# Decoder layer with latent attention, WKV and experts: the hand-over to the experts in a written order, first loads on POOL's queue, four half buffers for single z

## The reference, cut to what matters

```python
x = x + attention(layernorm(x))            # 16 sequences x 128 tokens x 256, 16 heads, latent 72, causal
x = x + sigmoid(layernorm(x)) * wkv(ctx)   # two scans over time of exp(ctx), each way
x = x + experts(layernorm(x))              # 8 experts, 512 wide, two of them for each token

# attention: K = V = x @ latent_w + latent_b;  q_h = x @ Wd_w[h] + Wd_b[h]
#   z_h = softmax(mask(q_h K^T / 4)) V;  out = concat(z_h) @ out_w + out_b
# experts: scores = x @ router_w.T, best two with gates
#   out += gate_e * ((silu(x @ w_gate[e].T) * (x @ w_up[e].T)) @ w_down[e].T)
```

## Time and the profile before

| | us |
|---|---|
| median of 3 runs (lowest, highest) | 666.33 (665.54, 668.06) |
| the profiled execution, its own time | 666.71 |
| its span | 665.0 |
| TensorE busy | 558.7 (84%) |
| VectorE busy | 418.1 (63%) |
| ScalarE busy | 366.6 (55%) |
| POOL busy | 328.6 (49%) |

### The profile page before, as it was taken

One profiled execution on the slowest core, in us unless ns is written; L12 is line 12 of the kernel. 1 busy time (PEld: TensorE's weight loads), 2 busy tenths in 40 slices (PEclk: granted clock), 3 DMA queues, 4 the chain that ended last, 5 costly groups with the idle time before them and its releaser, 6 DMA issues.

```text
span 665.0 us, 11259 instructions
## 1 busy us (share of the span) xinstructions
PE 558.7 (84%) x3778; PEld 489.2 (74%) x3778; DVE 418.1 (63%) x888; ACT 366.6 (55%) x997; POOL 328.6 (49%) x300
## 2 busy tenths in 40 slices
PE   1997869998979997999689567596299999999991
PEld 0885757776758876778567446596299999999991
DVE  4468475565876739856455744778167777777760
ACT  5276545756658544645364422665167677667651
POOL 3274635625245176632533441027656777766533
PEclk9999879999999998999798888799599999999997
DMA  7234444463444322523221165547578897888710
GB/s 233 82 56 67 56 61 76 62 90 51 63 88 99 51 43 51 102 73 61 42 87 31 28 200 177 147 116 141 146 203 220 230 225 220 227 218 230 182 34 0
DMA packets 55757, 75.92 MB, mean 114 GB/s; under 512 B 11730, under 2 KB 45140, under 8 KB 55444
## 3 DMA queue, kind: packets, MB, share of 16 engines
q1 hardware_dynamic: 45098, 64.90, 39.5%
q0 software_dynamic: 9856, 10.28, 9.1%
q10 hardware_dynamic: 746, 0.02, 0.1%
HBM read 48.90 MB, written 10.40 MB: 89 GB/s over the span
## 4 chain that ended last, share of the span: by engine, by line
PE 45%; DVE 20%; issue 12%; POOL 10%; ACT 7%; DMA 4%; another core or an unknown queue 1%; SPq 0%; POOLq 0%; ACTq 0%; DVEq 0%
PE P L842 22%; PE PO L842 9%; PE PO L951 4%; DVE ZT L1391 3%; ACT EB L1143 3%; PE P L920 3%; DVE small L1380 2%; POOL EB L1712 2%; POOL xs L1748 2%; DVE arena L1413 2%; PE P L938 2%; DVE arena L1415 2%; DMA qT<-qP 1%; PE P L996 1%; DMA arena<-wd 1%
## 5 line engine op out<-in xcount | busy, mean ns | idle before, releaser
L1143 ACT ACTIVATE EB<-P,small 128x128 f32<-128x128 f32 x256 | 90.6, 366 | 120.3 <-DVE small L1380 117.7
L842 PE MATMUL P<-GT,WF 128*128 128x256 f32 x1104 | 147.8, 292 | 7.4 <-DVE GT L1290 6.0
L1712 POOL TENSOR_TENSOR EB<-EB,small 128x512 f32<-128x512 f32 x64 | 75.7, 1183 | 153.6 <-DVE small L1384 153.5
L842 PEld LDWEIGHTS P<-GT,WF 128*128 128x128 f32 x1104 | 141.3, 199 | 8.4 <-DVE GT L1290 6.6
L1772 POOL DMA_INDIRECT out<-Y,TK x46 | 74.5, 1619 | 53.5 <-ACT Y L1229 43.5
L1762 POOL DMA_INDIRECT cxa<-xd,TK x46 | 64.2, 1396 | 60.3 <-DMA TK<-xs 51.5
L938 PE MATMUL P<-PT,V 128*72 128x512 f32 x128 | 68.4, 616 | 25.7 <-DVE ZT L1391 21.2
L920 PEld LDWEIGHTS P<-KT,qT 72*128 72x128 f32 x512 | 70.6, 201 | 9.3 <-DMA qT<-qP 5.8
L920 PE MATMUL P<-KT,qT 72*128 72x128 f32 x512 | 71.3, 284 | 5.0 <-DMA qT<-qP 4.6
L951 PE MATMUL PO<-Ow,zP 128*128 128x256 f32 x288 | 74.3, 399 | 0.0
L842 PE MATMUL PO<-WF,HR 128*128 128x256 f32 x552 | 70.0, 283 | 0.0
(11 more groups left out here) (186 smaller groups left out, 942.9 us busy)
## 6 DMA issues: line engine op xcount, KB each, us to landing
arena<-wf SPq DMA_DIRECT2D x36, 512.0 KB
WR<-wf SPq DMA_DIRECT2D x33, 512.0 KB
qT<-qP SPq DMA_DIRECT2D x63, 128.0 KB
zP<-ZT SPq DMA_DIRECT2D x80, 72.0 KB
zP<-ZT SPq DMA_DIRECT2D x96, 36.0 KB
X<-x SPq DMA_DIRECT2D x4, 512.0 KB, 5.8
cxa<-ctxin SPq DMA_DIRECT2D x4, 512.0 KB, 6.1
out<-X SPq DMA_DIRECT2D x3, 512.0 KB, 3.6
```

What stands on the lines that cost most here:

```text
L842: r = e.matmul(o, lt(a), rt_(b), start=start and n == 0, stop=stop and n == 2, skip_group_check=skip)
L1143: e.activation(EB[i][:, j, :], S[:, 128 * j:128 * j + 128], ACT.Exp, bias=NM[i][:, j:j + 1], accum_out=SM[i][:, j:j + 1]).then_inc(s_exp, 1)
L1712: e.tensor_tensor(EB[i][:, :, :], EB[i][:, :, :], SM[i].unsqueeze(2).broadcast_to([128, 4, 128]), ALU.mult).then_inc(s_prob, 1)
```

## The change

- The first three weight pieces (gw) and the first three lists (gtk) are loaded from POOL's queue with semaphores of their own. `lists` waits until turn 5 x 65 and emits them together with the first three gathers (before: after plan(0) on SP, with the gathers after the last unit).
- The 24 single units use the two ZT buffers as four halves, each with its semaphore (`z_home`).
- SHARE_LATE goes from 0.9 to 0.7, PACE_TILES from 0.5 to 0.1.
- After the last unit, tiles 0 and 1 and the last half group's norms, gate and route are emitted step by step; plan(1) is left to the planner. The tile loop starts at tile 2, and lists from 5 on are fetched from the beginning of tile 4.
- `up` is split in three steps: up (TensorE), si (ScalarE) and hd (VectorE).

```diff
-PACE, PACE_TILES = 1.0, 0.5
-LATE, SHARE_LATE, PACE_LATE = 52, 0.9, 0.6
+PACE, PACE_TILES = 1.0, 0.1
+LATE, SHARE_LATE, PACE_LATE = 52, 0.7, 0.6
...
+ZTWO = 4 * PAIRED
+
+
+def z_home(n):
+
+    z, nb = packing(n)
+    if nb == NB:
+        return z % 2, None, z // 2
+    return (z - ZTWO) % 4 // 2, (z - ZTWO) % 2, (z - ZTWO) // 4
...
-        if g == NG - 1:
-            yield from plan(1)
...
-        if b0 + nb == GB:
+        if nb == GB:
...
     def lists():
 
-        yield from rest(5)
+        while now[0] < 5 * (NU + 1):
+            yield -1
         for k in range(3):
-            load_w(0, k)
-        yield from rest(3)
+            emit("gw", 0, k)
         for j in range(3):
-            emit("ltk", j)
+            emit("gtk", j)
+        for j in range(3):
+            emit("lxg", j)
...
-              [(62, stage_e(3, 0, 2)), (NU + 3, stage_e(3, 2, 2))],
+              [(62, stage_e(3, 0, 2)), (NU + 3, plan(1))],
...
+    def product(j, n):
+        emit("up", j, n)
+        emit("si", j, n)
+        emit("hd", j, n)
...
-    finish(n, lambda: ("ltk", 2) in order and NG - 1 in w_done)
-    for j in range(3):
-        emit("lxg", j)
+    finish(n, lambda: ("lxg", 2) in order and ("tx", 3, 3, 0, 2, 1) in order and NG - 1 in w_done)
+
+    g, b0, nb = NG - 1, GB // 2, GB // 2
+    for k in range(3):
+        emit("lw", 1, k)
     split_w(0, 0)
     split_w(0, 1)
     emit("tg", 0)
-    for k in range(3):
-        load_w(1, k)
+    split_w(0, 2)
+    for j in (3, 4):
+        emit("ltk", j)
+        emit("lxg", j)
     emit("up", 0, 0)
+    split_w(1, 0)
+    emit("tg", 1)
+    emit("si", 0, 0)
+    emit("hd", 0, 0)
+    split_w(1, 1)
+    emit("sh", 0, 0)
     projections_of(B - 1)
     emit("add", NK - 1)
+    emit("bn", 2, g, b0, 0)
+    emit("agg", 2, g, b0, nb, True)
+    for i in range(3):
+        emit("rs", 2, g, b0, nb, i)
+    emit("up", 0, 1)
+    emit("nr", g, b0, nb)
+    split_w(1, 2)
+    emit("sig", g, b0, b0)
+    emit("si", 0, 1)
+    emit("x2", g, b0, b0, True)
+    emit("up", 1, 0)
+    emit("out", g, b0, nb)
+    emit("hd", 0, 1)
+    emit("si", 1, 0)
+    emit("bn", 3, g, b0, 0)
+    emit("agg", 3, g, b0, nb, True)
+    for i in range(3):
+        emit("rs", 3, g, b0, nb, i)
+    emit("nmb", 3, g, b0, nb)
+    emit("up", 1, 1)
+    emit("xn", 3, g, b0, 0)
+    emit("sh", 0, 1)
+    emit("xd", g, b0, nb)
+    emit("hd", 1, 0)
+    for k in range(2):
+        emit("tx", 3, g, b0, nb, k)
+    split_w(2, 0)
+    emit("sh", 1, 0)
+    for p in (0, 2):
+        emit("lg", g, 0, GB, p)
+    emit("lgc", g, 0, GB)
+    emit("si", 1, 1)
+    emit("dn", 0)
+    for name in ("r1", "r2", "ra"):
+        emit(name, g, 0, GB)
+    emit("tg", 2)
+    emit("hd", 1, 1)
+    emit("r3", g, 0, GB)
+    split_w(2, 1)
+    emit("rw", g, 0, GB)
+    for c in range(2):
+        for p in (0, 2):
+            emit("r4", g, 0, GB, c, p)
+    emit("sh", 1, 1)
 
     st.update(quick=True, pace=PACE_TILES, share=SHARE_TILES, gap=GAP_TILES)
-    fetched = [3]
+    fetched = [5]
...
-        while fetched[0] <= min(upto, NT - 1) and ready(fetched[0]):
+        while fetched[0] <= min(upto, NT - 1) and ready(fetched[0]) and upto > 6:
             emit("ltk", fetched[0])
             emit("lxg", fetched[0])
             fetched[0] += 1
 
-    for j in range(NT):
+    for j in range(2, NT):
...
-        if j:
-            emit("up", j, 0)
+        product(j, 0)
...
+        def tk_loaded(j):
+
+            return (s_gtk[j], 16) if j < 3 else (s_tk[j % 4], 16 * (j // 4 + (j % 4 == 3)))
...
+                    buf, half, _ = z_home(n)
                     c = slice(0, 128 * NB) if nb == NB else slice(128 * (b % NB), 128 * (b % NB) + 128)
+                    c_in = c if half is None else slice(128 * half, 128 * half + 128)
                     for j in range(4):
                         o = 8 * (4 * hq + j)
-                        e.dma_start(zP[k % 2][o:o + 8, :, c], ZT[z % 2][:, j, c]).then_inc(s_zd[z % 2], 16)
+                        e.dma_start(zP[k % 2][o:o + 8, :, c], ZT[buf][:, j, c_in]).then_inc(s_zd[buf] if half is None else s_zh[buf][half], 16)
...
+                if half is None:
+                    ve_.wait_ge(s_zd[buf], 64 * uses)
+                else:
+                    ve_.wait_ge(s_zd[buf], 64 * (ZTWO // 2))
+                    ve_.wait_ge(s_zh[buf][half], 64 * uses)
+                e.tensor_copy(ZT[buf][:, :, c:c + 128], YB[0:L, :].rearrange("p (h t) -> p h t", h=4)).then_inc(s_z, 1)
...
+            def load_first_w(j, k):
+                a, b = PARTS[k]
+                po.wait_ge(s_pe_, 1)
+                po.wait_ge(s_wb, total["wb"])
+                po.wait_ge(s_scan, 4 * total["w5"])
+                po.wait_ge(s_wsum, 5 * total["wa"])
+                v = e.value_load(PI[0:1, j:j + 1], min_val=0, max_val=NE - 1)
+                e.dma_start(WR[0][:, a:b], wf[bass.ds(v, 1), :, a:b].rearrange("a p n -> (a p) n")).then_inc(s_gw[k], 16)
+
+            def load_first_tk(j):
+                po.wait_ge(s_pr, 1)
+                for i in range(3):
+                    po.wait_ge(s_sc[i], SCATTERS)
+                po.wait_ge(s_fill, 48)
+                v = e.value_load(PI[0:1, NT + j:NT + j + 1], min_val=0, max_val=NE * CAP - TW)
+                e.dma_start(TK[:, j, :, :], xs[bass.ds(v, TW), :].rearrange("(p a) c -> p a c", a=2)).then_inc(s_gtk[j], 16)
```

More of the change, by code:

```diff
@@ L447, in schedule @@
         beside_turn(j + 3)
-        emit("up", j, 1)
+        product(j, 1)
         beside_turn(j + 3)
@@ L452, in schedule @@
         beside_turn(j + 3)
-        if j:
-            emit("dn", j - 1)
+        emit("dn", j - 1)
         beside_turn(j + 3)
@@ L653, in build @@
         s_zd = [sem(f"z_packed{i}") for i in range(2)]
+        s_zh = [[sem(f"z_packed_half{i}{j}") for j in range(2)] for i in range(2)]
         s_O, s_add = sem("projected"), sem("x1_added")
@@ L665, in build @@
         s_out = [sem(f"x2_stored{i}") for i in range(5)]
+        s_gtk, s_gw = [sem(f"first_tokens_loaded{i}") for i in range(3)], [sem(f"first_w_loaded{k}") for k in range(3)]
         s_tk = [sem(f"tokens_loaded{i}") for i in range(4)]
@@ L807, in load_tk @@
                 sp.wait_ge(s_fill, 48)
-                if j > 3:
-                    sp.wait_ge(s_tk[j % 4], 16 * (j // 4))
+                if j > 6:
+                    sp.wait_ge(*tk_loaded(j - 4))
                 v = e.value_load(PI[0:1, NT + j:NT + j + 1], min_val=0, max_val=NE * CAP - TW)
@@ L945, in project @@
                     pe.wait_ge(s_add, b // 2)
+                    z = packed_upto(b)
                     for j in range(2):
-                        pe.wait_ge(s_zd[j], 64 * ((packed_upto(b) + 1 - j) // 2))
+                        pe.wait_ge(s_zd[j], 64 * ((min(z, ZTWO) + 1 - j) // 2))
+                    for j in range(4):
+                        if z > ZTWO + j:
+                            pe.wait_ge(s_zh[j // 2][j % 2], 64 * ((z - ZTWO + 3 - j) // 4))
                     for a in range(2):
@@ L1195, in w_hi @@
                 i, (a, b) = j % 2, PARTS[k]
-                ac.wait_ge(s_wf[i][k], 16 * (j // 2 + 1))
+                if j == 0:
+                    ac.wait_ge(s_gw[k], 16)
+                else:
+                    ac.wait_ge(s_wf[i][k], 16 * (j // 2 + i))
                 if j == 0:
@@ L1224, in weigh @@
                 ac.wait_ge(s_dn, j + 1)
-                ac.wait_ge(s_tk[j % 4], 16 * (j // 4 + 1))
+                ac.wait_ge(*tk_loaded(j))
                 if j > 1:
@@ L1263, in scalar_program @@
                     rows_hi(*a)
-                elif name == "up":
+                elif name == "si":
                     silu(*a)
@@ L1386, in copy_mixed @@
             def copy_mixed(n):
-                z, nb = packing(n)
-                c = 128 * (UNITS[n][1] % NB)
+                buf, half, uses = z_home(n)
+                c = 128 * (UNITS[n][1] % NB if half is None else half)
                 ve_.wait_ge(s_Y, n + 1)
-                ve_.wait_ge(s_zd[z % 2], 64 * (z // 2))
-                e.tensor_copy(ZT[z % 2][:, :, c:c + 128], YB[0:L, :].rearrange("p (h t) -> p h t", h=4)).then_inc(s_z, 1)
+                if half is None:
+                    ve_.wait_ge(s_zd[buf], 64 * uses)
+                else:
+                    ve_.wait_ge(s_zd[buf], 64 * (ZTWO // 2))
+                    ve_.wait_ge(s_zh[buf][half], 64 * uses)
+                e.tensor_copy(ZT[buf][:, :, c:c + 128], YB[0:L, :].rearrange("p (h t) -> p h t", h=4)).then_inc(s_z, 1)
             def add_x1(i):
@@ L1646, in vector_program @@
                     rows_lo(*a)
-                elif name == "up":
+                elif name == "hd":
                     hidden(*a)
@@ L1752, in gather_rows @@
                 i = j % NX
-                po.wait_ge(s_tk[j % 4], 16 * (j // 4 + 1))
+                po.wait_ge(*tk_loaded(j))
                 for d in range(5 if phase(j) else 3):
@@ L1794, in gpsimd_program @@
                     scatter_slots(*a)
```

(4 more changed lines are left out.)

## The result

The changed kernel takes 668.9 us (median of 20 runs, 665.67 to 678.3), the kernel before on the same chip 665.81 (20 runs, 662.08 to 669.3): a ratio of 1.0057, 95% interval 1.0032 to 1.0082. The change makes the kernel 0.6% slower. The profiled execution took 671.36 us, its span is 669.7; before it was 666.71 and 665.0.

The account below looks back on a forecast made before the run. Only the hand-over, 387.0 to 477.3, has room; its wait chain sets tile 5's transposes. T0 14.8 later, A 16.2 later, then 12.7 saved: +3.6 on 666.3 gives 670 us, range 654 to 679.

Parts of the forecast that it names:

- tg 5: Start of TensorE's transposes of tile 5, after which nothing changes: 477.27 before, forecast 480.9.
- T0: Moment of the first gate matmuls, 400.70 before: forecast 415.5, 14.8 us later.
- A: Moment of the addition of x1 for the last two sequences, 409.60 before: forecast 425.8, 16.2 us later.
- A to tg 5: Stretch of normalise, gate, route, scatters, plan, list 5 and gather: forecast 55 us, 12.7 less than the 67.7 before.
- POOL's order: On POOL late in attention: last probabilities, three weight loads, three list loads, six gathers, then x2's addition, ending at 405.
- The loads on POOL: Six direct DMAs issued by POOL: 2.05 us each, 12.3 together, between 7 (SP's pitch) and 19.
- T0 to A: Stretch from gate matmuls to the x1 addition, tg 1 now before the last projection: forecast 10.3 us, 8.9 before.
- The net: Sum of all shifts at the start of tile 5's transposes: 3.6 us later, 480.9 against 477.3.
- The half buffers: End of attention: with loads off SP, copies 62 and 63 lose waits of 5.11 and 2.62, a gain of 4.2 us.
- The first rival: Much faster, 655 or 651 us, if x2's addition comes before the loads or doesn't hold copies 62 and 63; chance 0.18.
- the account of 0.9: Planner credit per turn kept at 0.9: x2 of (3, 0) due at turn 318, ahead of the lists' turn 325.

Follow-up runs that it names:

- pool_delay: The changed kernel with 16 clears of a scratch buffer on POOL ahead of the late addition of x2 for (3, 0): 675.54 us, ratio 1.0183.
- x2_dve: The changed kernel with the addition of x2 for the last group done by VectorE instead of POOL: 661.12 us, ratio 0.9958.
- lists_sp: share_09 with the first three weight pieces and lists issued by SP instead of POOL, at the same turn: 667.26 us, ratio 1.0026.
- list5_only: The changed kernel, share 0.7, with token list 5 and its gathers fetched one piece earlier: 666.96 us, ratio 1.0038.
- before_halves: The kernel before with the four half buffers alone, loads still on SP: 662.07 us, ratio 0.9956.
- x2_first: The changed kernel, share 0.7, with POOL's loads and gathers made to wait for the addition of x2 for (3, 0): 668.4 us, ratio 1.0078.
- share_09: The changed kernel with SHARE_LATE back at 0.9, everything else as changed: 657.0 us, ratio 0.9914.
- after: The changed kernel itself, against the kernel before: 668.9 us, ratio 1.0057.
- list5_early: share_09 with lists 5 and 6 and their gathers fetched from the beginning of tile 3: 653.17 us, ratio 0.982.
- loads_early: list5_early with POOL's three weight loads placed 11 to 13 planner turns earlier and its three list loads 7: 653.92 us, ratio 0.9838.
- sp_early: list5_early with the first weight loads and lists issued by SP at the turns of the kernel before: 658.49 us, ratio 0.9838.

## Why the prediction was right, and where its terms were not

The forecast was 670.0 within 654 to 679, slower; measured were 668.9 and a ratio of 1.0057. That it is slower is clear of noise, but not that it is slower by more than the 0.5% which the prediction took as its bound: the interval reaches from 0.3 to 0.8%, and the medians differ by 3.1 us, just under the 3.3. The mechanism is the one it described. That the sum came out within 1.2 us at tg 5 is in part luck: T0 was forecast 3.3 us too late and A to tg 5 4.8 us too short.

- **POOL's order** is the forecast one: probabilities, weight loads, list loads, gathers, addition of x2; bn 3 released by it after 13.19 us, near 404 by the forecast and 400.72 in the trace. That this is what holds T0 is shown by pool_delay (one for one) and by x2_dve (11.7 us back from the last probabilities on).
- **The loads on POOL** were mis-sized: 12.3 us in the sum, 8.3 from 383.82 to the first gather (392.08), and only 5.3 to the end of the last load; the other 3.0 is the wait for the first list to land. The rows are 0.54 to 0.63 long at a pitch of 1.15 to 1.2, which is the lower bound taken from SP's pitch; the value taken was drawn from POOL's indirect DMAs, and these are another kind. The rule of the Trainium skill that was weighed there (DMA: Bandwidth & Descriptors, section SWDGE vs HWDGE vs iDMA) puts plain transfers on SP or ACT. In the price of issuing the traces agree by a little (six loads took 6.1 us on SP and 6.7 on POOL); in the time of the kernel, lists_sp shows POOL the better queue by 7 to 10 us, because of what stood before the loads on SP.
- **T0 and T0 to A.** T0 came 3.3 earlier than forecast (412.16 against 415.5), about the 4.0 of this term; T0 to A was 10.1 against 10.3.
- **A to tg 5** was forecast at 55 (its last terms, 48.8, 1.3 and 5.6, in fact make 55.7, and those up to XN 11.7, not 11.9) and took 59.8. Three sizes failed. The first scatter came at A + 29.4 and not 26.7; this one is the slower clock of the profiled execution (in list5_only, at 26.6, it came as forecast). The eight scatters took 13.8 us and not 10.2, because four of the rows are 1.55 to 2.16 long and not 0.96; in the trace of before, five of the eight were 1.16 to 2.02 long already. They ended at A + 43.2 instead of 36.9, and tile 1's output additions stood behind them. And the sum let POOL add tile 2's output at once: the additions wait for those of tile 1 to land, 5.05 us, which no term had. That wait delayed the gather by less, about 3 us by my estimate: SP issued list 5 at 471.37 (A + 49.1, forecast 45.9), and in list5_only the gather starts 3.7 us after its list was issued, which would be 475.1 here instead of 478.07. Against all this the last gathers landed faster, 2.69 us (the forecast took the 5.6 of the earlier trace rows).
- **The net** was forecast as +3.6 at tg 5 and was +4.85. From there on nothing changed, as forecast.
- **The half buffers** were said to take away both waits, a gain of 4.2 us with the loads off SP. before_halves gives 3.4 us with the loads still on SP: for those waits the halves alone are enough, and the move of the loads is not needed.
- **The first rival** had one wrong condition. It said that the time would be 655 where the add comes first. x2_first did just this and took 668.4, since the loads then wait as the addition did. share_09, where the account of 0.9 places the product early as well, took 657.0.

So of the change's parts, the written hand-over is what helps: A to tg 5 takes 57.8 to 62.0 us in every kernel that has it with list 5 where the change put it, and 67.7 and 68.3 in the two that don't. (Part of that spread is TensorE's speed: in after, lists_sp and x2_dve the first scatter comes at A + 29.2 to 29.4, in the other four at 26.4 to 26.5.) No run has it alone, and PACE_TILES, which was changed with it, was never varied. The halves are worth 3.4 us on the kernel before. The share of 0.7 together with the loads on POOL costs 1.4%, some 9.5 us (after against share_09), more than either brings. Best measured is list5_early, 653.17 us (0.982), not distinguishable from loads_early and sp_early.

## What to carry to other kernels

When a step is moved to another engine's queue, look at what is already there and who waits for it, before the price of the issue itself: here six DMAs cost about the same on either queue, and their place was worth 7 to 10 us. Where two paths that end in one moment share a queue, swapping their order moves the wait and not the time; take one of them off the queue, or feed the shared step earlier. A load that is moved to an idle queue still shares the DMA engines with what is urgent. An earlier moment counts only when the next queue is ready for it: T0 was brought 5 us forward in one run, and the weights behind it on SP took most of it back.

## What the runs showed of the hardware

- An output addition by indirect DMA takes long to land: tile 1's second issue starts at 467.71, and its landing ends 5.80 us later; in share_09 it took 7.41. This kernel lets each addition wait for the one before it, and POOL stood 5.05 and 6.67 us. The 1.6 us that POOL's row shows is not its price in such a chain.
- A plain DMA issued by POOL with a register load took 0.53 to 0.64 us, about half of an indirect one (0.95), but at nearly the same pitch: mostly 1.15 to 1.2 against 1.26.
- Three weight loads during attention raised the DMA engines' busy share over 12 us from 0.10 to 0.55, and the projection that waits for the last pack of z issued in them started 3.0 us later.
- Indirect DMAs of one kind on POOL are mostly 0.95 long, but single ones took 2.0 to 3.7 us (the first gather in share_09 3.39, the fourth in sp_early 3.67, three of the last eight scatters 2.03 to 2.16). The long scatters are no chance: in all twelve kernels with the changed hand-over it is the third, sixth, seventh and eighth, each time with the same lengths within 0.02. What makes them long no run here tells.
- The granted clock after A differed between executions of the same order: 24 matmuls took 4.38 us in one and 3.12 in another (granted clock of the stretch 0.84 and 0.94).
